# A gated attention layer moved between the down products of the feed-forward stage ahead of it

## The reference

```python
# end of layer 1
out = rmsnorm(attn_out, postnorm_w)
x = gelu_tanh(out @ mlp_w1 + mlp_b1) @ mlp_w2 + mlp_b2 + residual     # 256 -> 1024 -> 256
# layer 2
q = x @ w_q.T; k = ctx @ w_k.T; v = ctx @ w_v.T
probs = softmax(q @ k.T / sqrt(256))
x = x + alpha * (probs @ v) @ w_o.T
# layer 3: two cross-attentions with 16 heads, and a second feed-forward part
```

## Time and profile before

| | |
|---|---|
| median of 3 runs | 1524.74 us (1524.71 to 1525.5) |
| the profiled execution's own time | 1526.7 us |
| its span, first to last instruction | 1524.9 us |
| TensorE busy, mean granted clock | 86% of the span, 0.914 of 2.4 GHz |
| VectorE, ScalarE, GpSimd busy | 51%, 36%, 30% |
| first feed-forward stage | 525.7 to 618.9 us |
| gated attention layer | 618.9 to 710.5 us |

### The profile page before, as it was taken

How to read it: one execution, slowest core, us unless ns; L and a number is a source line. 1 busy time by engine, 2 the same in 40 slices (tenths; PEclk the granted TensorE clock), 3 DMA queues, 4 the chain that set the end, 5 groups by cost and what they waited for, 6 DMA issues and landing times.

```text
span 1524.9 us, 21909 instructions
## 1 busy us (share of the span) xinstructions
PE 1317.6 (86%) x7584; PEld 861.5 (56%) x7584; DVE 772.2 (51%) x1613; ACT 556.5 (36%) x1030; POOL 452.7 (30%) x497
## 2 busy tenths in 40 slices
PE   5787874899988799777999899999999899996789
PEld 3676763455554488444555456665555456654667
DVE  6888861655665544222333465553333465545443
ACT  1344441255554545032333232222333222223443
POOL 3566654322301221010222223222222232223222
PEclk8888877799999899956999899999999899997899
DMA  7000005765650200000121100000111100000000
GB/s 246 2 0 0 0 1 91 107 97 84 91 77 13 115 1 1 0 0 0 57 66 61 43 1 0 0 0 13 58 57 57 55 0 0 0 0 1 14 14 28
DMA packets 36843, 55.39 MB, mean 36 GB/s; under 512 B 12518, under 2 KB 29478, under 8 KB 34470
## 3 DMA queue, kind: packets, MB, share of 16 engines
q1 hardware_dynamic: 34566, 53.70, 15.9%
q10 hardware_dynamic: 2208, 0.79, 0.2%
HBM read 45.05 MB, written 9.18 MB: 36 GB/s over the span
## 4 chain that ended last, share of the span: by engine, by line
PE 60%; DVE 5%; ACT 3%; issue 3%; POOL 1%; SPq 0%; DMA 0%; ACTq 0%; DVEq 0%; POOLq 0%
PE ps L1001 7%; PE ps L1026 7%; PE ps L838 5%; PE ps L937 4%; PE ps L854 4%; PE ps L941 4%; PE ps L949 4%; PE ps L958 4%; PE ps L855 2%; PE ps L953 2%; PE ps L726 2%; ACT pT L1069 1%; PE ps L1029 1%; PE ps L997 1%; PE ps L923 1%
## 5 line engine op out<-in xcount | busy, mean ns | idle before, releaser
L1488 DVE TENSOR_REDUCE nm<-ps 128x1 f32<-128x320 f32 x256 | 115.8, 486 | 81.1 <-PE ps L693 78.4
L1962 POOL TENSOR_TENSOR p<-p,sm 128x1024 f32<-128x1024 f32 x32 | 60.8, 1901 | 257.4 <-DVE sm L1696 257.4
L1001 PE MATMUL ps<-g,hT 128*128 (+1 forms) x256 | 127.6, 621 | 0.0
L1026 PE MATMUL ps<-v,pT 128*128 (+1 forms) x512 | 117.2, 382 | 1.7 <-DVE xr L1702 1.7
L693 PE MATMUL ps<-ks,qs 97*128 97x320 bf16 x256 | 77.4, 318 | 33.2 <-DVE nm L1488 15.8
L1069 ACT ACTIVATE pT<-ps 128x512 f32<-128x512 f32 (+1 forms) x80 | 39.0, 530 | 181.4 <-PE ps L1015 177.1
L1026 PEld LDWEIGHTS ps<-v,pT 128*128 128x128 f32 x512 | 94.7, 190 | 14.5 <-DVE xr L1702 2.1
L1072 ACT ACTIVATE pT<-ps 128x512 f32<-128x512 f32 x160 | 85.2, 603 | 46.6 <-PE ps L707 36.2
L1072 ACT ACTIVATE p<-p 128x1024 f32<-128x1024 f32 (+1 forms) x64 | 68.0, 1063 | 64.5 <-DVE p L1688 56.4
L854 PE MATMUL ps<-wb,hid_high 128*128 128x512 f32 x256 | 90.7, 398 | 0.0
L1633 DVE TENSOR_TENSOR br<-ps,bt 65x512 f32<-65x512 f32 x32 | 22.0, 687 | 134.0 <-ACT bt L1069 134.0
(11 more groups left out here) (238 smaller groups left out, 2997.1 us busy)
## 6 DMA issues: line engine op xcount, KB each, us to landing
bun_m<-in_heads SPq DMA_DIRECT2D x32, 522.0 KB, 3.5
ks<-k_parts SPq DMA_DIRECT2D x48, 160.0 KB, 8.1
qs<-q_parts SPq DMA_DIRECT2D x48, 128.0 KB, 7.4
q_parts<-qp SPq DMA_DIRECT2D x8, 384.0 KB, 11.6
k_parts<-kp SPq DMA_DIRECT2D x8, 384.0 KB, 10.9
w<-in_w SPq DMA_DIRECT2D x2, 1024.0 KB, 7.1
xr<-in_x SPq DMA_DIRECT2D x1, 2048.0 KB, 20.2
out<-xr SPq DMA_DIRECT2D x16, 128.0 KB, 1.7
```

Of the source, the lines that this page charges most:

```text
L1001: mm(ps[:, 2 * t + c, :], hT[t][:, kt, :], g3[:, kt, bass.ds(b, 1), c * 512:(c + 1) * 512], start=kt == 0, stop=False)
L1026: mm(o, pT3[half][:, n, :], v3[:, bass.ds(i, 1), 4 * half + n, :], start=half == 0 and n == 0, stop=False)
L1488: v.tensor_reduce(nm1[i % 2][:, t, h:h + 1], ps[:, u % 2, 0:KEYS1], X, ALU.max, negate=True).then_inc(D1t["maxima"].sem, 1)
```

## The change

The layer is no longer a stage. Its steps become moves, one letter each, capital for TensorE and small for ScalarE and VectorE, placed by a table between the down products: with chunk 0 the preparation, with chunk i the four tiles of chunk i - 1 ("a chunk behind"), three steps from tile to tile, and the tiles of chunk 3 after the last down product. A chunk has 16 such steps, eight for each pair of tiles, one for each f. TensorE does a step's moves ahead of the products of that f. ScalarE does all the moves of a chunk after its eight gelus and copies. VectorE does those of steps 0 to 7 ahead of the row sums of tiles 0 and 1 and those of steps 8 to 15 ahead of tiles 2 and 3. The hardware loop is unrolled, GpSimd's copy of the rows goes (TensorE reads `xr`), the copies of the preparation move from VectorE to ScalarE, and W is done in two halves. There is one bank for the transposed rows (6), one for the scores (7), and the transposed weights and the output use the up banks 0 and 1, so that the up products get waits on them. The three first loads of head weights wait until the preparation is done.

```diff
+        PREP2 = {0: "Kk", 3: "Qq", 6: "Vv", 9: "Ww", 12: "Ww"}
+        TILE2 = {0: "Xx", 2: "Sm", 3: "es", 5: "Tc", 6: "Oy"}
+        def step2(i, h):
+            if i == 0:
+                return [(move, h // 12) for move in PREP2.get(h, "")]
+            out = []
+            for t in reversed(range(QC)):
+                out += [(move, (i - 1) * QC + t) for move in TILE2.get(h - 3 * t, "")]
+            return out
+        STEPS2 = 16
...
             sp.dma_start(w2[:, :], io["w2"]).then_inc(dma_w2, 16)
+            sp.wait_ge(A2["values_out"].sem, A2["values_out"].end(1))
...
             def mlp_up(m, w, i, f):
+                if m == 0 and i >= 2 and f < 2:
+                    wait(*((A2["weights_turned"], D2["rows"])[f], (i - 1) * QC - 1))
                 wait(AM[m]["gelu"], i, f - 2)
...
+            def move2(move, k):                                    # TensorE
...
+                elif move == "X":
+                    wait(DM[0]["rows"], k // QC, k % QC)
+                    wait(A2["turned"], k - 1)
+                    if k == 0:
+                        wait(A2["values_out"], 0, 1)
+                    for kt in range(KT):
+                        last = tr(ps[:, 6, kt * P:(kt + 1) * P], xr[:, k, kt * P:(kt + 1) * P], ident)
+                    last.then_inc(E2["turned"].sem, 1)
+                elif move == "S":
+                    wait(A2["turned"], k)
+                    wait(A2["weights"], k - 1)
+                    for kt in range(KT):
+                        last = mm(ps[:, 7, 0:SC], x2T[k % 2][:, kt, :], k2[:, kt, k // QT_B, :],
+                                  start=kt == 0, stop=kt == KT - 1)
+                    last.then_inc(E2["scores"].sem, 1)
+                elif move == "T":
+                    wait(A2["weights"], k)
+                    wait(A2["weights_turned"], k - 1)
+                    wait(AM[0]["gelu"], min(k // QC + 1, NCH - 1), FT - 1)
+                    tr(ps[0:SC, 0, 0:P], p2[k % 2][:, :], ident).then_inc(E2["weights_turned"].sem, 1)
+                elif move == "O":
+                    wait(A2["weights_turned"], k)
+                    wait(D2["rows"], k - 1)
+                    mm(ps[:, 1, 0:D], pT2[k % 2][:, :], v2[:, k // QT_B, :], start=True, stop=True).then_inc(E2["out"].sem, 1)
...
             def mlp_down(m, w, i, first):
...
+                    if m == 0:
+                        for move, k in step2(i, FT * (first // 2) + f):
+                            move2(move, k)
                     for t in tiles:
...
-            with pe.Fori(0, B) as i:
...
+            for h in range(STEPS2):
+                for move, k in step2(NCH, h):
+                    move2(move, k)
...
+            def move2(move, k):                                    # ScalarE
...
+                elif move == "w":
+                    wait(E2["values_out"], 0, k)
+                    copy(v2[:, 4 * k:4 * k + 4, :].rearrange("p b n -> p (b n)"), ps[0:SC, 6:8, :].rearrange("p k n -> p (k n)"),
+                         scale=alpha[0:SC, :]).then_inc(A2["values_out"].sem, 1)
+                elif move == "x":
+                    wait(E2["turned"], k)
+                    wait(E2["scores"], k - 2)
+                    copy(x2T[k % 2][:, :, :], ps[:, 6, 0:D].rearrange("p (k n) -> p k n", k=KT)
+                         ).then_inc(A2["turned"].sem, 1)
+                elif move == "e":
+                    wait(D2["shift"], k)
+                    wait(E2["weights_turned"], k - 2)
+                    wait(D2["sum"], k - 2)
+                    exp(p2[k % 2][:, :], ps[:, 7, 0:SC], bias=sm2[k % 2][:, 0:1], scale=SCALE2
+                        ).then_inc(A2["weights"].sem, 1)
...
                 for i in range(NCH):                               # ScalarE, mlp_gelu
                     for f in range(FT):
...
+                    for h in range(0 if m else STEPS2):
+                        for move, k in step2(i, h):
+                            move2(move, k)
...
+            def move2(move, k):                                    # VectorE
+                sm = sm2[k % 2]
+                if move == "m":
+                    wait(E2["scores"], k)
+                    wait(A2["weights"], k - 2)
+                    wait(D2["rows"], k - 2)
+                    own(D2["maxima"], k, 0, v.tensor_reduce(sm[:, 3:4], ps[:, 7, 0:SC], X, ALU.max, negate=True))
...
                     for t in range(QC):                            # VectorE, mlp_rows
+                        for h in range(0 if m or t % 2 else STEPS2 // 2):
+                            for move, k in step2(i, STEPS2 // 2 * (t // 2) + h):
+                                move2(move, k)
                         rows = xr[:, i * QC + t, :]
                         wait(EM[m]["down"], i, t)
...
-            with pool.Fori(0, B) as i:
-                for t in range(2):
...
-                    g.tensor_copy(x2[t][:, :], xq(i, t)).then_inc(g2.sem, g2.did(f"x{t}"))
```

More of the change, by code:

```diff
@@ L370, in build @@
                        for k, per in steps.items()})
[L372 to L378, removed]
+        E2 = mlp_counts(E1, B, keys=("q", 1), keys_q=("k", 1), values=("v", 1), values_out=("max_turned", 2), turned=("pieces", 1),
+                        scores=("heads_turned", 1), weights_turned=("projected", 1), out=("normed_turned", 1))
+        A2 = mlp_counts(A1, B, keys=("q", 1), keys_q=("k", 1), values=("k_high", 1), values_out=("v", 2), turned=("max_high", 1),
+                        weights=("normed_turned", 1), weights_turned=("k_ctx_high", 1))
+        D2 = mlp_counts(G1, B, maxima=("q_rest", 1), shift=("k_rest", 1), sum=("q_mid", 1), inverse=("k_mid", 1), rows=("mask", 1))
         vbz = [sem(f"bias_values_zero{a}") for a in range(2)]
-        g2 = Steps(sem, "l2_pool", two("x%d"))
         EH = counting_on(E0, keys="q", values="scores", scores="turned_a", bias="turned_b", out="heads", rest="projected")
@@ L1052, in _ @@
                 if a == 0:
-                    pe.wait_ge(d2.sem, d2.end(B))
-                    pe.wait_ge(a2.sem, a2.end(B))
+                    for t in (DM[0]["rows"], AM[0]["gelu"]):
+                        pe.wait_ge(t.sem, t.end(NCH))
+                    for t in (D2["rows"], A2["weights_turned"]):
+                        pe.wait_ge(t.sem, t.end(NQ))
                 else:
@@ L1211, in mlp_columns @@
                 last.then_inc(AM[1]["xc"].sem, 1)
+            def move2(move, k):
+                if move in "kv":
+                    step = "keys" if move == "k" else "values"
+                    wait(E2[step], 0)
+                    for mt in range(KT):
+                        last = copy(t2[:, mt, :], ps[:, 6 + mt, :])
+                    last.then_inc(A2[step].sem, 1)
+                elif move == "q":
+                    wait(E2["keys_q"], 0)
+                    for mt in range(KT):
+                        last = copy(k2[:, mt, :, :], ps[:, 6 + mt, :].rearrange("p (b k) -> p b k", b=B))
+                    last.then_inc(A2["keys_q"].sem, 1)
+                elif move == "w":
[13 more added lines that the diff above has]
+                        ).then_inc(A2["weights"].sem, 1)
+                elif move == "c":
+                    wait(E2["weights_turned"], k)
+                    wait(E2["out"], k - 2)
+                    copy(pT2[k % 2][:, :], ps[0:SC, 0, 0:P]).then_inc(A2["weights_turned"].sem, 1)
             def mlp_gelu(m, w, loaded, func):
@@ L1324, in _ @@
                 if a == 0:
-                    act.wait_ge(e2.sem, e2.end(B))
-                    act.wait_ge(d2.sem, d2.end(B))
+                    for t in (DM[0]["rows"], EM[0]["down"]):
+                        act.wait_ge(t.sem, t.end(NCH))
+                    for t in (E2["out"], D2["rows"]):
+                        act.wait_ge(t.sem, t.end(NQ))
                 else:
@@ L1988, in _ @@
                 if a == 0:
-                    pool.wait_ge(e2.sem, e2.end(B))
-                    pool.wait_ge(d2.sem, d2.end(B))
+                    pool.wait_ge(DM[0]["rows"].sem, DM[0]["rows"].end(NCH))
+                    for t in (E2["out"], D2["rows"]):
+                        pool.wait_ge(t.sem, t.end(NQ))
                 else:
```

121 lines of the change are left out of this document (54 added, 67 removed).

## The result

The changed kernel takes 1488.78 us (median of 4, 1483.86 to 1489.9) against 1524.72: a ratio of 0.9753, 95% interval 0.974 to 0.9767, or 36 us less. The forecast was 1485 with a range of 1478 to 1494. The profiled execution has a time of 1489.9 and a span of 1488.1 us.

A forecast was written before the change was run, and what follows sets the result against it. Bound: the attention layer's three-engine chain, waiting at a low clock, 93.2 us on the critical path. Terms 17.5 + 16.5 + 5.4 + 13.9 = 53.3, so 39.9 less: about 1485 us, range 1478 to 1494.

The forecast's parts named there:

- 1, preparation in chunk 0: Chunk 0: K, Q, V and W products between down products at full clock, copies hidden: 17.5 us.
- Term 2: TensorE's own products of twelve attention tiles between down products, 1.37 us a tile at full clock: 16.5 us.
- Term 3: TensorE's in-order waits in chunks 1 to 3, at scores products S0 (0.7) and S1 (1.1): 5.4 us in all.
- Term 4: Drain: tiles 12 to 15 behind the last down product, clock low after two tiles: 13.9 us, bounds 12 to 18.
- more waits: Rival: small slacks tip, each tile waits 0.5 to 1 us, drain at loop's pace: about 1491 to 1497; chance 0.17.
- the dearer switch: Rival: ScalarE's table switch also drains for 1.28 us, delaying S1 in each of three chunks: 1488.8 us; chance 0.05.
- the fall of the clock: Rival: down products of the three interleaved chunks run at 1.2 GHz, 34 us more: 1519 us; chance 0.03.
- Fewer waits and a warm drain: Rival: chunk waits and drain at their lower bounds, 0 and 12 us: 1477.5 us in total; chance 0.14.
- The one of the other side: Rival: TensorE stands through each tile's whole chain, 4.9 us a tile, 58.8 for twelve: 1538 us, slower; chance 0.03.
- the threshold of 3.8: Mean wait per tile, in us over twelve tiles, above which the change was forecast to turn slower.

The follow-up runs named there:

- the one with both edits: Changed kernel with the exponential ahead of the copy in ScalarE's list and the output product over 128 rows: 1477.13 us, ratio 0.969 to the kernel before.

## Why the prediction was right

By its own terms, in us of the stage:

| term | forecast | measured | from |
|---|---|---|---|
| 1, preparation in chunk 0 | 17.5 | 17.9 | 43.03 - 25.09 |
| 2, products of 12 tiles | 16.5 | 19.9 | 3 x (7.61 - 0.97) |
| 3, waits of three chunks | 5.4 | 2.9 | 3 x (0.78 + 0.19) |
| 4, drain | 13.9 | 10.2 | 662.69 to 672.87 |
| sum | 53.3 | 50.9 | |
| saved of 93.2 | 39.9 | 42.2 | 184.78 - 142.56 |

The mechanism was right in each: within the chunks the waits stood where I had walked them, at S0 and S1 and nowhere else, there was none at Q, V, W, O or T, and the switch back to gelu cost nothing. The sizes were off in three terms (3.4 too small, 2.5 and 3.7 too large). That they cancel but for 2.4 us is luck.

Term 2 was 3.4 us too small: the rows I took for the output product were of one over 128 rows, and ours has 64; the experiment gives 0.39 us a tile for that, 4.7 us in twelve. The scores, at 0.43 us, were cheaper than the 0.55 I took.

Term 3 was 2.5 too large. S0 waited 0.19 in place of 0.7, since the copy x0 ended 0.1 us after S0 was due and my signals were too long; S1 0.78 in place of 1.1. By the experiments S1's wait was worth 1.02 a chunk, so 3 x 0.24 = 0.7 us of what the table has in term 2 belongs here.

Term 4 was 3.7 too large, and 10.2 lies under the 12 that I had as its lower bound. I let the clock fall after two tiles; it held for about 8 us and the tiles went at 1.75 us. In the kernel with 128 rows and in the one with both edits it fell sooner (drains of 12.5 and 11.1 us), so the drain isn't a constant.

The total came out 3.8 us above the forecast though the stage came out 2.3 below. In the pair of traces the stage saves 42.2, of which the later start takes back 4.6 and the part behind the heads 0.8; the change doesn't set the 4.6, as the other kernels' traces show. The second measurement of the same kernel gave 1485.74.

What I had wrong was the emphasis. I wrote that waiting and the low clock would go, gave no shares, and said of products put between down products that only latency is saved. The sum adds up what remains, so it couldn't show where the gain comes from. The experiments split the 42.2 us: 10.2 for the loop's table loads, 9.0 for the order with three tiles in flight and whatever else the unrolled layer has otherwise, 7.5 for the preparation inside chunk 0 (its copies' waits in the main), and 15.5 for putting the tiles between down products, of which 12 x (2.83 - 7.61 / 4) = 11.1 are a tile at 1.2 GHz against one at 2.4. I take the rest of the 15.5 to be the gap at the start and the few drained tiles at the high level.

The rivals: more waits, the dearer switch and the fall of the clock did not occur. Fewer waits and a warm drain did, for terms 3 and 4: they measured 2.9 + 10.2 = 13.1 us, close to the 12 of that rival and far from my 19.3. Its total of 1477.5 did not come, since term 2 was too small and the first up product came late. The one of the other side does occur if the stagger is taken out, but not by the price I gave it. It had 4.9 us of wait a tile; the experiment has 24.0 / 12 = 2.0 of listed wait, which alone lies under the threshold of 3.8. A tile costs (45.97 - 29.84) / 4 = 4.0 us more than in the changed kernel (chunks 1 and 2 begin at 575.20 and 621.17), because the low clock makes the down products longer too, and that makes it slower than before.

## What to carry to other kernels

A latency-bound stage of small products can cost twice, once in waits and once in TensorE's clock, and here the second stayed when the waits were hidden; look at the granted clock of the stage, and put such products between dense ones (or, failing that, give them company). Ahead of a hardware loop, see that ScalarE's table set on entry is the one at the end of a turn; here each of eight turns loaded it again, 10.2 us in all. When moves are threaded through in-order lists, walk one period engine by engine; the order of two moves on the engine that switches tables was worth 3 us here, and filling the row dimension of a small product another 1.58 in each of three chunks; 6.9 us came of both together.

## What the runs showed of the hardware that I had not expected

A product over 64 rows between products over 128 cost 0.39 us beside its own passes (twelve tiles, 1.58 us a chunk): the weight loads on both sides of it weren't hidden. That the row count is the reason is shown by the experiment; whether 32 or 96 rows do the same wasn't tried.

TensorE can read as busy 30.00 of 30.00 us and stay at a clock of 0.50, and 0.85 us of extra product in a tile of 2.8 kept the clock at 1.00 for 36 us, so that the tile took 2.40. The busy share of the profile didn't tell the two apart.

The table load in straight code ran ahead of the waits of its activation (0.02 us after the copy before it), while in the loop it came after them (0.79 us after the transposes began). Why the two differ isn't shown.
